# Value products of an attention window moved from the odd to the even score pairs

## The reference

```
x = x + 0.5*ffn0(layernorm(x))          # one 128x128 matrix in effect
x = x + attn0(layernorm(x))             # 16 heads of 8; the softmax attention is applied twice:
                                        #   state = softmax(state @ k.T) @ v, from state = q
x = x + 0.5*ffn0(layernorm(x))
x = x + 0.5*moe(layernorm(x))           # 8 experts, top 2, and a shared one
x = x + attn1(layernorm(x))             # 16 heads of 8, block mask
x = x + 0.5*moe(layernorm(x))
```

## Time and profile before

| what | value |
|---|---|
| median of 3 runs | 3903.79 us (3903.47 to 3909.41) |
| the profiled execution's own time | 3903.75 us |
| its span, first to last instruction | 3902.0 us |
| TensorE matmuls busy | 3366.3 us, 86% |
| VectorE busy | 2383.3 us, 61% |
| ScalarE busy | 2158.5 us, 55% |
| GpSimd busy | 1063.0 us, 27% |
| mean granted TensorE clock | 0.911 of full |

### The profile page before, as it was taken

One profiled execution on the slowest core, in us unless ns is written; L12 is line 12 of the kernel. 1 busy time (PEld: TensorE's weight loads), 2 busy tenths in 40 slices (PEclk: granted clock), 3 DMA queues, 4 the chain that ended last, 5 costly groups with the idle time before them and its releaser, 6 DMA issues. The chain is left out here.

```text
span 3902.0 us, 54943 instructions
## 1 busy us (share of the span) xinstructions
PE 3366.3 (86%) x20118; PEld 1699.3 (44%) x20118; DVE 2383.3 (61%) x5217; ACT 2158.5 (55%) x2817; POOL 1063.0 (27%) x2225
## 2 busy tenths in 40 slices
PE   4778888898989989898998989898998989898886
PEld 2224343344444434444444445444453444444553
DVE  2335575666757666675757666675766667575563
ACT  1444566565555656555566656556665655564432
POOL 3122213141412323141332414132231414121311
PEclk6678799898989989898999989899998989899997
DMA  1000000000000000000001000000000000000100
GB/s 37 0 1 28 4 28 4 28 28 31 28 31 25 7 28 29 31 28 31 25 7 45 12 31 29 31 27 24 34 4 31 28 31 28 28 25 11 48 28 30
DMA packets 71257, 95.81 MB, mean 25 GB/s; under 512 B 40304, under 2 KB 58160, under 8 KB 70864
## 3 DMA queue, kind: packets, MB, share of 16 engines
q1 hardware_dynamic: 70992, 92.29, 7.2%
HBM read 82.76 MB, written 4.78 MB: 22 GB/s over the span
## 5 line engine op out<-in xcount | busy, mean ns | idle before, releaser
L712 ACT ACTIVATE probs<-ps 128x1024 f32<-128x1024 f32 x1536 | 1574.8, 1025 | 1006.0 <-PE ps L576 970.3
L875 DVE TENSOR_REDUCE negmax<-ps 128x2 f32<-128x1024 f32 x1024 | 1251.8, 1223 | 723.2 <-PE ps L617 713.7
L576 PE MATMUL ps<-qT,kT 32*128 32x512 f32 x3072 | 826.0, 533 | 374.0 <-ACT probs L712 354.8
L593 PE MATMUL ps<-probs,v 128*32 128x512 f32 x6144 | 907.2, 666 | 0.1
L576 PEld LDWEIGHTS ps<-qT,kT 32*128 32x128 f32 x3072 | 305.5, 195 | 1083.8 <-ACT probs L712 733.4
L1083 POOL TENSOR_TENSOR xe<-xT_m,G 128x512 f32<-128x512 f32 x288 | 368.7, 1283 | 1135.9 <-PE ps L654 910.3
L654 PE MATMUL ps<-xe,w_sb 128*128 128x256 f32 x2304 | 650.9, 408 | 12.1 <-POOL xe L1083 8.3
L617 PE MATMUL ps<-kT,qT 32*128 32x512 f32 x2048 | 555.2, 537 | 73.1 <-DVE negmax L875 73.0
L654 PEld LDWEIGHTS ps<-xe,w_sb 128*128 128x128 f32 x2304 | 404.9, 195 | 249.0 <-issue 177.4
L742 ACT ACTIVATE th<-ps 128x256 f32<-128x256 f32 x576 | 221.9, 385 | 335.1 <-PE ps L654 333.6
L940 DVE SCALAR_TENSOR_TENSOR th<-th,ps 128x256 f32<-128x256 f32 x576 | 238.8, 415 | 254.7 <-ACT th L742 242.3
(11 more groups left out here) (168 smaller groups left out, 2773.2 us busy)
## 6 DMA issues: line engine op xcount, KB each, us to landing
G<-gates_dram SPq DMA_DIRECT2D x96, 768.0 KB, 6.2
v<-v_tok SPq DMA_DIRECT2D x256, 18.0 KB, 1.9
X<-in_x SPq DMA_DIRECT2D x16, 256.0 KB, 8.1
out<-X SPq DMA_DIRECT2D x16, 256.0 KB, 2.3
w_sb<-in_w SPq DMA_DIRECT2D x1, 1152.0 KB, 5.5
w_sb<-in_w SPq DMA_DIRECT2D x1, 576.0 KB, 6.3
gates_dram<-gT SPq DMA_DIRECT2D x32, 18.0 KB
wqkv<-in_wqkv SPq DMA_DIRECT2D x2, 192.0 KB, 2.4
```

The costliest lines, as they stand in the source:

```text
L576: nc.tensor.matmul(ps[:, B_ST + h, :], kT[a][rows, g * S + kc * P:g * S + (kc + 1) * P], qT[a][rows, g * S:(g + 1) * S], start=True, stop= ...
L593: ins = nc.tensor.matmul(ps[ROWS * j:ROWS * (j + 1), B_UT, :], v[:, at:at + ROWS], probs[:, n % QUADS, j, :], start=(kc == 0), stop=(kc == ...
L712: nc.scalar.activation(probs[:, quad % QUADS, j:j + 2, :], ps[:, B_ST:B_ST + 2, :], ACT.Exp).then_inc(sem["exp_done"], 1)
L875: nc.vector.tensor_reduce(negmax[job_no(kind, b, g) % 2][:, tc, 2 * half:2 * half + 2], ps[:, B_SM:B_SM + 2, :], AX_X, ALU.max, negate=Tru ...
```

## The change

The position of the value products goes from 3.3 to 2.02 of the slot count.

```diff
     for i in range(WIN):
         t.at(start + i, "st", kind, b, g, i)
     for kc in range(TC):
-        t.at(start + 2 * kc + 3.3, "pv", kind, b, g, kc)
+        t.at(start + 2 * kc + 2.02, "pv", kind, b, g, kc)
     t.at(start + 10.2, "uts", kind, b, g)
     t.at(start + 11.2, "turn", kind, b, g)
```

## The result

The changed kernel takes 3931.46 us in the median of 11 runs (3904.09 to 3947.58), the kernel before 3908.06 us (3901.70 to 3913.42, 11 runs). The ratio is 1.0052, with a 95% interval of 1.0029 to 1.0075: 0.5% slower, where 0.5% faster was forecast. The time is outside the forecast's range of 3842 to 3926.

A forecast was written before the change was run, and what follows sets the result against it. TensorE runs a chain of slots, each ending at the later of the score-exp loop (floor 1.70 us) and its own work. Terms 20 + 7 - 25 - 26 + 10 - 5 = -19 us against 3903.75 give 3885 us, range 3842 to 3926.

The forecast's parts named there:

- (e): Clock in pairs with a transpose: less idle time lets it rise sooner, 15 of 694 us at half clock saved, -5 us.
- The sign that was named for it: Mean clock of the run: stays within 0.90 to 0.92; the prediction is wrong if it leaves that band.
- the clock stays low for longer: Rival, 5%: odd-slot bunches that raise the clock are split, 100 us longer at low clock, +36 us, 3921 us.
- (b): Slots at half clock: separating value products from transposes saves 1.05 us in 31 pairs, six `m_gu` pairs lose 1.2: -25 us.
- (a): Other work in the slot at full clock: even slots slightly fuller, +20 us, and +7 us in slots 16 to 31.
- (d): First value products of a window: a new wait for the copy, 0.21 us each, +3 to +19 us, taken as +10.
- (c): Max pairs waiting for VectorE, mainly odd slots 9, 45, 61, 73: moved value products shorten waits, -39 to 0, taken as -26.
- The rule of the slot: Value products cost the slot's other TensorE work less 0.27 us, no less than 0 and no more than 1.
- The Trainium skill's rule on idle gaps: Ties the clock's fall to long idle gaps between matmul bursts; by it (b) and (e) are nil, sum 30 us higher.

The follow-up runs named there:

- experiment 7: Against the kernel before, only the value products of even slots 18, 20 and 26 of each turn move: 3848.03 us, ratio 0.9832.
- experiment 14: The changed kernel with the value products of slots 30, 32 and 34 left in their odd slots: 3872.67 us, ratio to the kernel before 0.9893.
- experiment 15: The changed kernel with the value products of slots 22 and 42 left in their odd slots: 3855.29 us, ratio to the kernel before 0.9851.
- experiment 10: The changed kernel with the value products of slots 22, 30, 32, 34 and 42 left in the odd slots: 3801.74 us, ratio to the kernel before 0.9725.
- experiment 8: The changed kernel with one more, overwritten 128x256 matmul ahead of the transposes in slots 19, 21 and 27: 3897.83 us, ratio to the kernel before 0.9948.
- experiment 2: The changed kernel, but the first value products of each window stay at 3.3 and the others move: 3915.48 us, ratio to the kernel before 1.0018.
- experiment 3: Against the kernel before, only the value products of even slots 16 to 34 of each turn move: 3963.60 us, ratio 1.0125.
- experiment 4: Against the kernel before, in turns 3 to 14 all value products move except those of slots 16 to 35: 3906.05 us, ratio 0.9991.
- experiment 5: Against the kernel before, value products take the emptier slot of each pair, 17 even slots of a turn: 3725.17 us, ratio 0.9515.
- experiment 12: Against the kernel before, only the first value products of each window move to the even slot: 3896.53 us, ratio 0.9957.
- experiment 11: The kernel of experiment 5 with an overwritten 128x256 matmul in slots 19, 21 and 27: 3722.65 us, ratio to the kernel before 0.9511.

## Why the prediction was wrong

The step that failed is **(e), the clock**. It assumed 15 us less at half clock; the runs have about 91 more, which is +31 us instead of -5. The sign that was named for it came: the mean clock left the band of 0.90 to 0.92, with a median of 0.898. The price of time at half clock was right: 36% assumed, 34% measured over eleven runs. The case "the clock stays low for longer" was among the rivals, with 100 us and 3921 us, close to what came, but with a chance of 5%. Its mechanism, odd bunches that raise the clock being split, is refuted by experiment 7: splitting them takes 151 us off the half-clock time.

Term (e) looked at the pairs of slots with a transpose (18 to 27), and (b) took the clock behind them as the old trace had it. In slots 16 to 29 the forecast's direction is right, with 7.0 us a turn less at half clock. What the runs show in its place is 11.0 us a turn more in slots 30 to 35, where value products and expert steps now stand in one slot, and 86 us more in turns 0 to 2 and 15 to 17, against 60 in the twelve middle turns together. Of slots 16 to 35 the forecast had 7 - 25 - 5 us, which is -1.8 a turn over 13 turns; the trace has +2.5. Experiments 14, 15 and 10 take the half-clock time from 802 to 728, 667 and 608 us by leaving full even slots out, and experiment 8 brings it down to 678 by added work. Why the clock stays low there is open: the single slots don't add up to the whole (experiments 2, 3 and 4).

The work terms **(a) to (d)** summed to -14 us, and the rest column has -9. That they agree is in part luck: the -25 of (b) is time saved in slots at half clock, part of which the rest leaves out by its definition. Outside slots 16 to 35, (a), (c) and (d) come to about 0 a turn (1.3 - 2.0 + 0.8), and the trace has -1.2.

- **(a)** The rule of the slot held. Slots with an even `m_gu` went from 1.70 to 2.4 to 2.8 us (2.49 forecast, more where a max pair is late), their odd neighbours to between 1.64 and 1.76. Applied per slot instead of summed, it found experiment 5, at 3725 us where the pairs gave 3720, with some help from the clock.
- **(b)** Pairs 18 and 20 gave back 2.0 and 1.3 us a turn and pair 26 1.1. But I counted only six pairs with an `m_gu` in the even slot at half clock, those of the old trace. With the change, slot 30 is at half clock in every one of turns 3 to 14 and slot 32 in nearly all; there the extra is 2.5 and 3.1 us. The term depended on the clock being where it was before.
- **(c)** was right in its places: slot 9 fell from 4.10 to 2.11 (2.4 forecast), slot 8 rose to 2.75 (2.65), and slot 66 rose by 1.8, as 1.0 of (a) and 0.8 of (c) make it. The total of weight-load waits fell only to 107.9 us, not to 70 or 80. I put that down to small waits that came back behind short odd slots, but did not count them.
- **(d)** The wait appeared at line 721, where it was forecast, at 0.3 to 0.7 us in five slots (26, 42, 74, 82 and 90) instead of 0.2. Part of that is a misread copy. The forecast took 0.60 us for it, and 1.05 for one that value products hold up. But in both traces all 64 copies of L1 windows take 1.02 to 1.06 us and the 128 others 0.59 to 0.65, although with the change no value products stand just ahead of any. The copies of slots 26, 42 and 82 are L1's. Experiment 12 has the whole move of first groups at -2 us of rest, so +10 was too much for the sum, and the wait in slot 42 is worth about 0.5 us a turn there.

The Trainium skill's rule on idle gaps (TensorE: Matmul & The Clock Gate, section "Why this matters for your kernels") was set aside because the clock was low with gaps of 1.2 us; the traces agree with setting it aside. In turns 3 to 14 the longest time without a matmul or weight load, in the half-clock stretches and just ahead of them, is 1.36 us before and 1.25 us with the change. The Trainium skill's statement that activity releases the throttle (same page, section "What's actually happening") agrees with experiments 8 and 11, where added matmuls took 124 and 49 us off the half-clock time. It does not tell which slots matter, and nor do I know it fully: why leaving out slots 22 and 42 takes off more half-clock time than leaving out 30 to 34 is open, as is how much of it is chance in when the clock changes. That half-clock time varies by 127 us from run to run of one kernel fits a kernel on the edge between the levels; it was not tried separately.

## What to carry to other kernels

Where an engine's work is laid out in slots with a floor (here an exp loop of 1.70 us), count each piece of work as the slot's other work less the room in it, and choose per piece; moving all pieces by one rule only trades full slots for other full slots (+1.3 us a turn), while choosing gave 4.9%. Before forecasting a move of TensorE work, look at how much of the span is at half clock and price it from the runs themselves: here 0.34 us per us, enough that 90 us of it outweighed everything else. When runs of one kernel spread by 1%, set span against mean clock first; one line through the points separates what the change costs from what the clock does, as far as half-clock time has the same price in both kernels. And when an instruction has two lengths in a trace, look for what tells the long ones from the short ones before putting it down to a wait.

## What was not expected of the hardware

Adding a matmul of 128x256 in three slots of a turn made the kernel faster by 34 us, since it took half-clock time from 802 to 678 us. The granted clock of one and the same kernel varied from 0.894 to 0.909 between runs, and the span with it from 3945.8 to 3902.3 us. The copy of 128x512 (line 721) has two lengths, and not because value products hold it up. In the trace of before, this S1 copy waits for them and still takes 0.60 us, while the L1 copy of the earlier trace rows has 1.05:

```profile
1813.82 0.60 ACT L721 ACTIVATE uts<-ps 128x512 f32<-128x512 f32 x1 [0.97 <-PE ps L593]
```

With the change, this L1 copy, ahead of the value products of slot 42, starts 2.5 us after the last ones that it has to wait for and still takes 1.03:

```profile
2127.73 1.03 ACT L721 ACTIVATE uts<-ps 128x512 f32<-128x512 f32 x1
```

In the code the copy of an L1 window writes its 512 columns in another order (`rearrange` on `dst` and `source`), the others don't. That this order is what makes it longer was not tried by itself.
